# A gated-attention kernel in which the expert of a token is chosen after the product with the states and no longer before it

## The reference

```python
x = x + layernorm(linear_attention(layernorm(x)))       # 16 heads of 32, relu(q), relu(k)
x = x + layernorm(gated_layer(layernorm(x)))            # 8 heads of 64, 4 experts
```

```python
def chunk_gla(q, k, v, gk):       # per chunk of 64 tokens
    g = cumsum(gk); qg = q * exp(g); kg = k * exp(-g)
    o_intra = tril(qg @ kg.T) @ v
    o_inter = qg @ S              # S: state before the chunk
    S = S * exp(g_last) + k_out.T @ v
    return o_intra + o_inter
o_dense  = chunk_gla(q1, k1, v, gk1)
o_sparse = sum over e of chunk_gla(q2 * p_e, k2 * p_e, v, gk2 * mask_e)   # p_e is 0 off expert e
o = rms_norm_per_head(o_dense + o_sparse) * norm_w * silu(g)
return o @ Wo
```

## Time and profile before

| | before |
|---|---|
| median of three runs | 2854.69 us |
| the profiled execution | 2854.88 us |
| its span, first to last instruction | 2853.0 us |
| TensorE busy | 2726.3 us (96%) |
| VectorE busy | 1860.9 us (65%) |
| ScalarE busy | 1680.7 us (59%) |
| GpSimd busy | 1354.2 us (47%) |
| mean granted clock of TensorE | 0.984 |

### The profile page before, as it was taken

One profiled execution on the slowest core, in us unless ns is written; L12 is line 12 of the kernel. 1 busy time (PEld: TensorE's weight loads), 2 busy tenths in 40 slices (PEclk: granted clock), 3 DMA queues, 4 the chain that ended last, 5 costly groups with the idle time before them and its releaser, 6 DMA issues.

```text
span 2853.0 us, 57155 instructions
## 1 busy us (share of the span) xinstructions
PE 2726.3 (96%) x21232; PEld 1728.3 (61%) x21232; DVE 1860.9 (65%) x3686; ACT 1680.7 (59%) x3345; POOL 1354.2 (47%) x1006
## 2 busy tenths in 40 slices
PE   6999799999999999999879997999999999999997
PEld 3444466666666666666534444666666666666665
DVE  4442477777777777777544425777777777777774
ACT  4333466666666666666434325666666666666664
POOL 2894254544445555544412242544445555444444
PEclk9999899999999999999889998999999999999998
DMA  5120100000000000000021101000000000000000
GB/s 185 63 92 34 38 23 22 22 22 22 22 22 31 24 22 22 22 22 22 19 90 63 59 34 38 23 22 22 22 22 27 28 22 22 22 22 22 22 22 12
DMA packets 48376, 97.49 MB, mean 34 GB/s; under 512 B 5376, under 2 KB 5376, under 8 KB 47680
## 3 DMA queue, kind: packets, MB, share of 16 engines
q1 hardware_dynamic: 37008, 68.44, 7.4%
q10 hardware_dynamic: 9792, 17.83, 1.7%
q0 software_dynamic: 1520, 10.50, 1.0%
HBM read 63.19 MB, written 33.55 MB: 34 GB/s over the span
## 4 chain that ended last, share of the span: by engine, by line
PE 93%; ACT 4%; DVE 1%; issue 1%; POOL 1%; DMA 0%; POOLq 0%; DVEq 0%; SPq 0%; ACTq 0%
PE psum L303 16%; PE psum L304 15%; PE psum L305 15%; PE psum L456 10%; PE psum L557 6%; PE psum L428 5%; PE psum L445 4%; PE psum L465 4%; PE psum L418 4%; PE psum L312 2%; ACT ogT L747 2%; PE psum L357 2%; PE psum L356 2%; PE psum L437 1%; PE psum L329 1%; PE psum L531 1%
## 5 line engine op out<-in xcount | busy, mean ns | idle before, releaser
L977 POOL TENSOR_TENSOR region<-region,mb 128x512 f32<-128x512 f32 x256 | 322.8, 1297 | 73.3 <-ACT region L630 72.9
L1010 POOL TENSOR_TENSOR region<-region,decay 64x1280 f32<-64x1280 f32 x128 | 298.0, 2328 | 117.8 <-DVE decay L1224 112.6
L995 POOL TENSOR_TENSOR region<-region,kfac 128x512 f32<-128x512 f32 x64 | 66.7, 1042 | 579.7 <-DVE kfac L1208 579.7
L456 PE MATMUL psum<-region 128*128 128x128 f32 x2560 | 302.9, 278 | 11.7 <-POOL region L977 11.7
L456 PEld LDWEIGHTS psum<-region 128*128 128x128 f32 x2560 | 294.7, 194 | 12.0 <-issue 12.0
L303 PE MATMUL psum<-wb,region 128*128 128x512 f16 x768 | 291.9, 380 | 3.0 <-DVE mb L1173 3.0
L304 PE MATMUL psum<-wb,region 128*128 128x512 f16 x768 | 292.0, 380 | 0.0
L305 PE MATMUL psum<-wb,region 128*128 128x512 f16 x768 | 291.8, 380 | 0.0
L969 POOL TENSOR_TENSOR region<-region 128x1024 f32<-128x1024 f32 x64 | 146.7, 2292 | 288.5 <-DVE region L1324 230.9
L990 POOL TENSOR_SCALAR region<-region,m 128x512 f32<-128x512 f32 x256 | 172.3, 692 | 198.5 <-DVE hm L1157 122.4
L1324 DVE SCALAR_TENSOR_TENSOR region<-psum,region 128x512 f16<-128x512 f32 x64 | 44.3, 692 | 261.9 <-ACT region L809 261.9
(11 more groups left out here) (231 smaller groups left out, 7357.0 us busy)
## 6 DMA issues: line engine op xcount, KB each, us to landing
region<-x_in SPq DMA_DIRECT2D x128, 256.0 KB, 2.7
q_cols<-region ACTq DMA_DIRECT2D x64, 256.0 KB, 2.3
region<-q_cols SPq DMA_DIRECT2D x64, 256.0 KB, 3.0
out_rows<-region SPq DMA_DIRECT2D x60, 256.0 KB, 2.0
region<-wb_in POOLq DMA_DIRECT2D x1, 3072.0 KB, 12.3
region<-wqkv_in SPq DMA_DIRECT2D x4, 512.0 KB, 6.7
region<-wqkv_in POOLq DMA_DIRECT2D x2, 1024.0 KB, 5.7
region<-wproj_in POOLq DMA_DIRECT2D x2, 1024.0 KB, 7.5
```

The lines of the kernel that those rows point to most:

```text
L456: last = mm(bank[7][:, pr * P:(pr + 1) * P], q, state[:, pr, path, :], start=(pr == 0 and path == 0), stop=False, skip_group_check=True)
L977: last = nc.gpsimd.tensor_tensor(qm[:, e, :, :], q2T, mb[:, e, :].unsqueeze(1).to_broadcast([P, PAIRS, P]), ALU.mult)
L1010: nc.gpsimd.tensor_tensor(state[h, :, :, h], carry[h, :, :, :], decay[h, :, :].unsqueeze(3).to_broadcast([D2, PAIRS, PATHS, D2]), ALU.mult ...
```

## The change

The states of the experts are stored compactly: per pair of heads a row of 128 partitions (the two heads above each other) and four experts of 64 columns (`statex`), with no empty blocks. The dense state keeps its block form (`state0`). `inter` multiplies the unmasked q2 of one head (64 rows) with all four experts' states at once (256 columns), in two halves of four products, which go to banks 2 and 3 and to banks 0 and 1. The dense product and `intra` still add up in bank 7, in an order of the heads that fits (`by_row`; the weights Wgb and Wo are permuted on the host to match).

The choice follows on VectorE (`back_select`): each token is a partition here, so each of the four results is multiplied with a 0 or 1 of the token (`m4`) and added, four operations per half. `back_join` adds bank 7. The squares and the norm read this sum from SBUF. The masks `mb` and the masked queries `qm` are gone, on VectorE and GpSimd.

Because the results need four banks, the banks are dealt anew: logits and k move from bank 0 to 2, the label's row to bank 7, k2 from 1 to 3, the second running sum from 2 to 3, the linear attention from 3 to 0. k2 now stands behind `intra`, q2 behind the transposes of og. The low halves of the second-level products take all 128 rows of weights (before, 64), and so does the bias of y. On ScalarE the high half of the log gates goes ahead of the squares, and the exponential of k2 behind them. On VectorE the maximum of k2 and its difference move behind the log sigmoid.

The diff, cut to its core:

```diff
-        qm = cut(NEXP, PAIRS, P, own=1)
         am1, am2 = cut(2, PAIRS, P, own=1), cut(2, PAIRS, P, own=1)
-        state = cut(PAIRS, PATHS, P, own=1)
-        carry = cut(PAIRS, PATHS, D2, own=1)
         sil, x1 = cut(2, C, own=1), cut(2, C, own=1)
-        loaded_at = cursor[1]
+        state0, statex = cut(PAIRS, P, own=1), cut(PAIRS, NEXP * D2, own=1)
+        carry0, carryx = cut(PAIRS, P, own=1), cut(PAIRS, NEXP * D2, own=1)
+        osum = cut(C, own=1)
...
-                mm(bank[3], ones16[0:HALF, :], bias16[0:HALF, :], start=True, stop=False)
+                mm(bank[0], ones16[:, :], bias16[:, :], start=True, stop=False)
...
-                pe.wait_ge(S("ldiff_ok"), cur(n))
-                mm(bank[0][:, 0:P], ones16[:, :], lab_i[:, :], start=True, stop=True).then_inc(S("rx_pe"), 1)
+                pe.wait_ge(S("low_ok"), cur(n))
+                mm(bank[7][:, 2 * P:3 * P], ones16[:, :], lab_i[:, :], start=True, stop=True).then_inc(S("rx_pe"), 1)
...
-                h = slice(0, LORA) if which < 3 else slice(LORA, P)
                 mm(out, low[:, which, :], ws[:, 0, k, :], start=True, stop=False)
-                return mm(out, low[h, which, :], ws[h, 1, k, :], start=False, stop=True)
+                return mm(out, low[:, which, :], ws[:, 1, k, :], start=False, stop=True)
...
-            def project_k2(n):
-                pe.wait_ge(S("v_ok"), cur(n))
-                second(bank[1], 3, 4).then_inc(S("k2_pe"), 1)
-
-            def project_k(n):
-                pe.wait_ge(S("mb_ok"), cur(n))
+            def project_k2(n, back):
+                pe.wait_ge(S("carry_ok"), prev(n))
+                if back:
+                    pe.wait_ge(S("sel_ok"), (n - 1) * 8 + 4)
+                second(bank[3], 3, 4).then_inc(S("k2_pe"), 1)
+
+            def project_k(n, back):
+                pe.wait_ge(S("ldiff_ok"), cur(n))
+                if back:
+                    pe.wait_ge(S("sel_ok"), (n - 1) * 8 + 4)
                 for g in range(KT):
-                    mm3(bank[0], lambda x: xnT[:, x, g, :], lambda x: wb[:, x, g, C:2 * C], g == 0, g == KT - 1)
+                    mm3(bank[2], lambda x: xnT[:, x, g, :], lambda x: wb[:, x, g, C:2 * C], g == 0, g == KT - 1)
 
             def project_q2(n):
                 pe.wait_ge(S("ls_ok"), cur(n))
-                second(bank[4], 2, 3)
+                second(bank[4], 2, 3).then_inc(S("q2_pe"), 1)
 
             def project_q1(n):
+                pe.wait_ge(S("ls_ok"), cur(n))
                 wide(n, 5, 0, "q1_pe")
...
-            def inter(n):
+            by_row = bank[7].rearrange("p (f o r d) -> p f o r d", f=2, o=2, r=2)
+
+            def inter(n, front):
+                pe.wait_ge(S("state_ok"), cur(n))
+                pe.wait_ge(S("q2T_ok"), cur(n))
+                pe.wait_ge(S("am1_ok"), cur(n))
+                pe.wait_ge(S("carry_ok"), cur(n))
+                if front:
+                    pe.wait_ge(S("ldiff_ok"), cur(n + 1))
+                for half, done in ((0, "ia_pe"), (1, "ib_pe")):
+                    if half and front:
+                        pe.wait_ge(S("v_ok"), cur(n + 1))
+                    for r in range(2):
+                        for odd in range(2):
+                            h = slice(odd * D2, odd * D2 + D2)
+                            last = mm(psum[:, 2 - 2 * half + odd, r * 256:r * 256 + 256], q2T[h, 2 * half + r, :],
+                                      statex[h, 2 * half + r, :], start=True, stop=True)
+                    last.then_inc(S(done), 1)
                 pe.wait_ge(S("out_ok"), prev(n))
-                pe.wait_ge(S("state_ok"), cur(n))
-                pe.wait_ge(S("qm_ok"), cur(n))
+                if front:
+                    pe.wait_ge(S("same_ok"), cur(n + 1))
                 for pr in range(PAIRS):
-                    for path in range(PATHS):
-                        q = q1T[:, pr, :] if path == 0 else qm[:, path - 1, pr, :]
-                        last = mm(bank[7][:, pr * P:(pr + 1) * P], q, state[:, pr, path, :],
-                                  start=(pr == 0 and path == 0), stop=False, skip_group_check=True)
+                    last = mm(by_row[:, pr // 2, :, pr % 2, :], q1T[:, pr, :], state0[:, pr, :].rearrange("p (o d) -> p o d", o=2),
+                              start=(pr == 0), stop=False, skip_group_check=True)
                 last.then_inc(S("inter_pe"), 1)
...
-                ac(osq[:, :], bank[7], ACT.Square).then_inc(S("osq_ok"), 1)
+                ac(osq[:, :], osum, ACT.Square).then_inc(S("osq_ok"), 1)
...
-            def back_qm(n):
-                pool.wait_ge(S("q2T_ok"), cur(n))
-                pool.wait_ge(S("mb_ok"), cur(n))
-                pool.wait_ge(S("state_ok"), cur(n))
-                pool.wait_ge(S("inter_pe"), prev(n))
-                for e in range(NEXP):
-                    last = nc.gpsimd.tensor_tensor(qm[:, e, :, :], q2T, mb[:, e, :].unsqueeze(1).to_broadcast([P, PAIRS, P]), ALU.mult)
-                last.then_inc(S("qm_ok"), 1)
...
-                for odd, done in ((0, "state_half"), (1, "state_ok")):
-                    h = slice(odd * D2, odd * D2 + D2)
-                    if odd:
-                        pool.wait_ge(S("state_half"), n + 1)
-                    nc.gpsimd.tensor_tensor(state[h, :, :, h], carry[h, :, :, :],
-                                            decay[h, :, :].unsqueeze(3).to_broadcast([D2, PAIRS, PATHS, D2]),
-                                            ALU.mult).then_inc(S(done), 1)
+                nc.gpsimd.tensor_tensor(state0, carry0, decay[:, :, 0].unsqueeze(2).to_broadcast([P, PAIRS, P]), ALU.mult)
+                nc.gpsimd.tensor_tensor(statex.rearrange("p a (e d) -> p a e d", e=NEXP), carryx.rearrange("p a (e d) -> p a e d", e=NEXP),
+                                        decay[:, :, 1:PATHS].unsqueeze(3).to_broadcast([P, PAIRS, NEXP, D2]),
+                                        ALU.mult).then_inc(S("state_ok"), 1)
...
             def back_carry(n):
-                for odd in range(2):
-                    h = slice(odd * D2, odd * D2 + D2)
-                    last = ve.tensor_tensor(carry[h, :, 1:PATHS, :], psum[h, 2:4, :].rearrange("p a (r e d) -> p (a r) e d", r=2, e=NEXP),
-                                            state[h, :, 1:PATHS, h], ALU.add)
+                for half in range(2):
+                    last = ve.tensor_tensor(carryx[:, 2 * half:2 * half + 2, :], bank[3 * half].rearrange("p (r c) -> p r c", r=2),
+                                            statex[:, 2 * half:2 * half + 2, :], ALU.add)
                 last.then_inc(S("carry_ok"), 1)
+
+            def back_select(n, p):
+                dve.wait_ge(S("osq_ok"), prev(n))
+                dve.wait_ge(S("on_ok"), prev(n))
+                for half in range(2):
+                    dve.wait_ge(S(("ia_pe", "ib_pe")[half]), cur(n))
+                    to = osum[:, half * 256:half * 256 + 256].rearrange("p (h d) -> p h d", h=H2 // 2)
+                    of = psum[:, 2 - 2 * half:4 - 2 * half, :].rearrange("p b (r e d) -> p (b r) e d", r=2, e=NEXP)
+                    for e in range(NEXP):
+                        if e == 0:
+                            step_ = ve.tensor_scalar(to, of[:, :, e, :], m4[:, p, e:e + 1], None, ALU.mult)
+                        else:
+                            dve.wait_ge(S("sel_ok"), n * 8 + half * 4 + e)
+                            step_ = ve.scalar_tensor_tensor(to, of[:, :, e, :], m4[:, p, e:e + 1], to, ALU.mult, ALU.add)
+                        step_.then_inc(S("sel_ok"), 1)
+
+            def back_join(n):
+                dve.wait_ge(S("o_pe"), cur(n))
+                dve.wait_ge(S("sel_ok"), n * 8 + 8)
+                ve.tensor_tensor(osum, bank[7], osum, ALU.add).then_inc(S("osum_ok"), 1)
...
-                dve.wait_ge(S("qm_ok"), prev(n))
-                for e in range(NEXP):
-                    last = ve.tensor_scalar(mb[:, e, :], row, float(NEXP - e), None, ALU.is_equal)
-                last.then_inc(S("mb_ok"), 1)
```

More of the change, by code:

```diff
@@ L311, in den @@
                 for g in range(KT):
-                    last = mm(bank[3][:, g * P:(g + 1) * P], kden[:, g, :], qb[:, p, g, :], start=True, stop=True)
+                    last = mm(bank[0][:, g * P:(g + 1) * P], kden[:, g, :], qb[:, p, g, :], start=True, stop=True)
                 last.then_inc(S("den_pe"), 1)
@@ L414, in transposes @@
                 pe.wait_ge(S("sil_ok"), cur(n))
-                for src, where, ready in ((q1g, 5, "q1g_ok"), (k1g, 0, "k1g_ok"), (q2g, 4, "q2g_ok"), (k2g, 6, "k2g_ok")):
+                for src, where, ready in ((q1g, 5, "q1g_ok"), (k1g, 2, "k1g_ok"), (q2g, 4, "q2g_ok"), (k2g, 6, "k2g_ok")):
                     pe.wait_ge(S(ready), cur(n))
@@ L1280, in step @@
                 if back:
+                    back_join(m)
+                if front:
+                    front_kmax(n)
+                if back:
                     back_norm(m)
                 if front:
```

(3 more changed lines are left out.)

121 lines of the change are left out of this document (63 added, 58 removed).

## The result

The changed kernel takes 2901.0 us (median of four runs, 2894.36 to 2915.34), the kernel before 2854.31 beside it (2853.55 to 2855.26). The ratio is 1.017, with a 95% interval of 1.0127 to 1.0213: slower, by 47 us. The profiled execution took 2894.36 us, with a span of 2892.5; it is the fastest of the four, and what follows accounts for its 39.5 us over the span before.

What follows compares the result with a forecast made beforehand. TensorE's own queue was taken to bound the second pass. The profiled 2854.9 us, +7 for sixty longer tiles, -4 for batch edges, +4 for clock falls gave 2862 us; likeliest case 2845 to 2880, whole range 2830 to 2915.

Steps and rivals of the forecast that it cites:

- rival (a): Clock falls in TensorE's new pause before og's transposes, 1.5 us each in half the tiles: 2905 us; chance 0.22.
- TensorE's new products: Eight 64-row, 256-column state products on TensorE, overlapping in separate array halves: 1.87 us, shape changes about 0.1 each.
- rival (c): The 64-row products on TensorE do not overlap: tile 34.9, 2910 us; chance 0.06 together with other new waits.
- TensorE's work saved, 2.25 us a tile: TensorE per tile: 4.52 - 0.90 - 1.87 - 0.2 + 0.7 = 2.25 us less work; 2711 us if TensorE stayed the bound.
- The first half of the products is there at 6.75: First four state products reach VectorE 6.75 us after the tile's start, so VectorE waits 0.5 us.
- The selection, 3.75 us: Eight 256-column VectorE selections ahead of og, about 0.475 us each, two halves of four: 3.75 us, done at 10.50.
- TensorE waits 2.3 us: TensorE reaches og's transposes at 16.9, og is done at 19.15: 2.3 us of waiting per tile, tile 34.05.
- Two to three falls of the clock, +4: Clock allowance in the forecast sum: two or three falls add 4 us to the kernel.
- Edges, -4: First and last steps of the batches, outside the full loops: together 4 us saved.
- The room is 1.29 us per tile, no more: Kernel before: og's last half done at 1017.84, its transposes begin at 1019.13, leaving 1.29 us of room per tile.
- Rival (b): Selections on VectorE shorter, 0.43 us each with wait, 3.3 in all: 2821 us, or 2838 for half; chance 0.24.
- Rival (d): Full TensorE gain, 2711 us, if og weren't late; needs VectorE's row wrong by over 2 us; chance 0.03.

Runs made afterwards that it cites:

- the first experiment: Eight useless 128x512 products put ahead of og's transposes on TensorE in the changed kernel: 2870.64 us, ratio 1.0062 to the kernel before.

## Why the prediction was right in its direction and 39 us short

The forecast was 2862, the result is 2901. It lies in the range of 2830 to 2915 and on the side that had 0.50, but outside the likeliest case's own range of 2845 to 2880, and close to the 2905 of rival (a). That closeness is luck in part: (a) reckoned thirty falls of the clock on a shorter tile. Of the 39 us, about 16 are the tile, 14 the falls of the clock, 3 the edges, and 7 lie between the profiled execution, the fastest of the four, and their median. By the prediction's own steps:

- **TensorE's new products.** Right. The eight of 64 rows were put at 1.87 and 0.1 for the change of shape; they take 1.92 (1017.34 to 1019.26), so the two halves of the array do work side by side, and rival (c) is out.
- **TensorE's work saved, 2.25 us a tile.** A little low, in the term for the 64-row products of the second level. The text spoke of six and took a tenth for each; the tile has three and the bias, with 0.21 each, 0.86 in all against 0.7. The slip in the count did little harm, because each of these products is two changes of shape. It made no difference to the tile either, since TensorE did not bound.
- **The first half of the products is there at 6.75.** The first selection begins at 7.01. The label's product came at 5.52 instead of 5.46, and from the first of the eight to the selection it took 1.27 (1017.34 to 1018.61), where 0.94 for four products, 0.1 for landing and 0.05 for waking had been taken.
- **The selection, 3.75 us.** It took 3.91. One operation is 0.48, as taken. The first of each half was counted with 0.45 and stands 0.51 to 0.52 ahead of the next, which makes up most of the difference; the others stand 0.52 apart and not 0.505. The overlap behind each half was put at 0.09 and is 0.08.
- **From there to og, 8.65 us.** Right (8.64, from 1022.52 to 1031.16), with the squares wait of 0.45 (0.4 forecast). og is done at 19.56 instead of 19.15, all of it from the two steps above.
- **TensorE waits 2.3 us.** It waits 2.56. It is there at 17.06 (forecast 16.9), and the rest is og's 0.4. From the transposes to the next tile it takes 14.70 (1.74 + 13.04 = 14.78 forecast). The tile is 34.31 instead of 34.05, 60 x 0.26 = 16 us more.
- **Two to three falls of the clock, +4.** This is the step that failed. There were eleven in the profiled execution, +18 us, and by clock and time perhaps more in two others. The text named the mechanism, its price (1.5 us each; measured 1.4 to 1.7) and a pause from which it would decide, about 2.1. No run bears out such a limit: with 2.56 in every tile the clock fell in 11 of 60, with 2.35 in six. The pause was forecast at 2.3, beyond that point, and yet the forecast kept all but two or three falls out of the likeliest case, having seen the clock bear several short pauses around 335. Those were several short ones and not one of 2.5, so they were weak evidence against it. Rival (a) with half the tiles was too much for this execution (11 of 60) and perhaps not far off for the slowest, which by an estimate from its time had about 24. The Trainium skill, TensorE: Matmul & The Clock Gate, section HAM oscillation, speaks of such a loop of work and wait whose rounds each start slow; here every tile has the pause and only 11 of 60 a slow stretch, in eight of them 1.2 to 1.4 us behind the pause's end, so the runs agree with it in kind and not in extent.
- **Edges, -4.** About -1. In the last step TensorE waited 3.87 for the carry and 5.47 for og, where before it was 5.83 and 4.6. With the useless products of the first experiment the edges come to -7; by that, some 6 us of the saving went into more time at the low clock there, such as 337.2 to 340.6 in the first batch's first step.
- **"The room is 1.29 us per tile, no more".** Wrong as it stands. The twelve useless masks show that at least 2.4 fit in. The sum did not suffer, since its steps carried the wait for the squares (1.37 before, 0.4 forecast) apart from that sentence; but whoever had judged by the sentence alone would have put the cost of any work on VectorE about a microsecond per tile too high, as I did in the expectation for the twelve.
- **Rival (b)** needed 0.43 per selection with its wait; the trace has 0.52, and 0.49 as the mean of the eight. Rival (d) would have needed VectorE's row wrong by 2 us; it was right within 0.4.

Shown by experiments: VectorE's row bounds (a shorter row and another order shortened the tile, more or less work on TensorE left it at 34.30), and the long pause goes with the falls of the clock: filled to 0.83 at the same tile of 34.30, none was left in the loops. Not settled: what picks the tiles that lose the clock. It isn't chance alone, for the low stretches begin at 511, 822, 856 and 894 us in the first batch and at 2232, 2542, 2576 and 2614 in the second, with the same 311, 34 and 38 us between them. Not settled either is whether the other three runs lost their time in the same way, as they have no trace. Whether the banks dealt anew cost anything was not tried by itself; the tile's balance leaves no more than about 0.1 us for it.

## What to carry to other kernels

When work moves from the engine that bounds to one that looks half idle, lay out that engine's row of operations up to the result that is waited for, with the waits inside it as room of their own; its busy share says nothing about it. After such a move look at the order again before the amount: the same instructions in another order were worth 110 us here, twice the loss and more. A pause of TensorE of some 2.5 us in each round can cost more than its length, since the clock may be low behind it (here in 11 of 60 rounds, for some 1.6 us each), and then even useless products in the pause make the kernel faster.

## What the runs showed of the hardware that was not expected

- Each 64-row product of 512 columns among full ones cost 0.21 us more than a full one, though it does half the work: about 0.1 in front of it and 0.1 behind. The full shape was faster here (-52 us), though its added rows are not empty: in the second level they hold the product of the two low halves, which the 64-row product leaves out, and the bias is spread over twice the rows.
- A selection on VectorE is 0.22 us long with 4 columns in each partition and 0.48 with 256. One that waits for the one before it starts 0.26 and 0.51 to 0.52 behind it; without that wait, one of 256 columns starts 0.39 to 0.40 behind.
- Pauses of 2.56 us a tile went with a low clock in 11 of 60 tiles, pauses of 2.35 in six, and pauses of 1.25, 0.82 and 0.47 with none, in one traced execution each. The granted clock was 0.50 in the whole of such a stretch, as in 1238.3 to 1241.7, with 1.00 on both sides, and most of them began over a microsecond behind the pause.
